# A fused linear-attention and FFN kernel: order of the opening's work, engine of the FFN weight's sums, and one bias addition a tile

## The reference, cut to what matters

```python
def _feature_map(x): return jax.nn.elu(x) + 1.0

# block 1: causal linear attention, 16 heads of 32, a running state kv and ksum per sequence
qkv = ln(x) @ W_attn + b_attn
q, k, v = split(qkv); q, k = _feature_map(q), _feature_map(k)
kv = kv + k[..., :, None] * v[..., None, :];  ksum = ksum + k     # token by token
y = (q . kv) / (q . ksum + 1e-6)
x = x + y @ W_proj + b_proj
# block 2: one linear layer on values rounded to fp8 e4m3
x = x + float16(fp8(ln(x))) @ float16(fp8(weight)).T + bias
```

## Time and profile before

| | |
|---|---|
| median of 3 runs | 955.94 us (952.33 to 960.21) |
| the profiled execution | 953.16 us |
| its span in the trace | 951.4 us |
| TensorE busy | 922.6 us (97%) |
| VectorE, ScalarE, GpSimd busy | 731.3, 747.3, 639.3 us |
| granted TensorE clock, mean | 0.998 |

### The profile page before, as it was taken

One profiled execution on the slowest core, in us unless ns is written; L12 is line 12 of the kernel. 1 busy time (PEld: TensorE's weight loads), 2 busy tenths in 40 slices (PEclk: granted clock), 3 DMA queues, 4 the chain that ended last, 5 costly groups with the idle time before them and its releaser, 6 DMA issues.

```text
span 951.4 us, 44839 instructions
## 1 busy us (share of the span) xinstructions
PE 922.6 (97%) x19533; PEld 491.2 (52%) x19533; DVE 731.3 (77%) x1405; ACT 747.3 (79%) x1362; POOL 639.3 (67%) x711
## 2 busy tenths in 40 slices
PE   7898999999999999999999999999999999999985
PEld 4354455555555555555555555555555555555553
DVE  7898778787786877778687687777778687676785
ACT  6787687887869688787877868788787868878864
POOL 5559777866767767776766777677676676654533
PEclk9999999999999999999999999999999999999999
DMA  8826554565464655564456555556566446553421
GB/s 270 139 44 116 96 119 94 101 119 93 100 125 93 100 119 96 98 119 98 99 116 106 93 113 109 100 104 113 90 109 115 95 103 120 90 93 70 69 71 51
DMA packets 252420, 99.12 MB, mean 104 GB/s; under 512 B 232384, under 2 KB 233408, under 8 KB 252224
## 3 DMA queue, kind: packets, MB, share of 16 engines
q1 hardware_dynamic: 252224, 96.25, 52.3%
HBM read 22.81 MB, written 16.78 MB: 42 GB/s over the span
## 4 chain that ended last, share of the span: by engine, by line
PE 87%; DVE 5%; POOL 2%; issue 2%; ACT 2%; SPq 1%; DMA 1%; POOLq 0%; DVEq 0%; ACTq 0%
PE R L245 74%; PE S L245 13%; DVE st L665 1%; DVE raw L704 1%; POOL st L944 1%; SPq L1168 1%; DVE qk L681 1%; POOL xn L946 1%; DMA yt<-yhl 0%; POOL xs L991 0%; DVE v L693 0%; POOL raw L977 0%; PE R L249 0%; DMA x2t<-x2b 0%; DVE wl L807 0%
## 5 line engine op out<-in xcount | busy, mean ns | idle before, releaser
L245 PE MATMUL R<-xt,wh 128*128 128x512 f16 x1024 | 304.6, 379 | 3.6 <-ACT rel L469 2.7
L681 DVE SCALAR_TENSOR_TENSOR qk<-qk,rel 128x512 f32<-128x512 f32 x128 | 112.9, 884 | 121.1 <-ACT rel L469 121.1
L457 ACT ACTIVATE raw<-qk 64x512 f32<-64x512 f32 x256 | 160.8, 628 | 49.2 <-PE S L245 46.0
L245 PE MATMUL R<-xt,wl 128*128 128x512 f16 x512 | 193.6, 379 | 0.0
L998 POOL TENSOR_TENSOR yhl<-y,yhl 128x512 f16<-128x512 f32 x60 | 70.1, 1168 | 146.4 <-ACT yhl L457 146.3
L245 PE MATMUL R<-wh,xt 128*128 128x512 f16 x512 | 158.0, 379 | 0.7 <-issue 0.7
L944 POOL TENSOR_TENSOR st<-st,half 128x1 f32<-128x1 f32 x128 | 94.1, 735 | 96.0 <-DVE st L670 95.4
L704 DVE TENSOR_TENSOR raw<-S,causal 64x1024 f32<-64x1024 f32 x128 | 155.8, 1217 | 2.0 <-PE S L245 1.1
L245 PEld LDWEIGHTS R<-xt,wh 128*128 128x128 f16 x1024 | 96.2, 98 | 116.7 <-ACT rel L469 3.4
L245 PE MATMUL R<-wph,yt 128*128 128x512 f16 x512 | 132.0, 380 | 5.1 <-ACT yt L457 3.2
L466 ACT ACTIVATE qk<-R,bqk,wm 128x512 f32<-128x512 f32 x128 | 98.8, 772 | 32.5 <-PE R L245 32.0
(11 more groups left out here) (95 smaller groups left out, 1410.3 us busy)
## 6 DMA issues: line engine op xcount, KB each, us to landing
xs<-in_L_attn_x SPq DMA_DIRECT2D x64, 256.0 KB, 3.3
out<-xs SPq DMA_DIRECT2D x64, 256.0 KB, 2.4
raw<-in_L_attn_W_attn SPq DMA_DIRECT2D x2, 1024.0 KB, 9.5
raw<-in_L_attn_W_attn SPq DMA_DIRECT2D x2, 512.0 KB, 5.7
xs<-in_L_attn_W_proj SPq DMA_DIRECT2D x4, 256.0 KB
raw<-in_L_ffn_weight SPq DMA_DIRECT2D x1, 1024.0 KB, 17.3
raw<-raw SPq DMA_TRANSPOSE x63, 3.7
x2t<-x2b SPq DMA_TRANSPOSE x62, 2.5
```

The lines of the kernel that those rows point to most:

```text
L245: return e.matmul(out, a, b, start=start, stop=stop, skip_group_check=True)
L457: return e.activation(out, in_, ACT.Copy, **more)
L681: e.scalar_tensor_tensor(qk[j % 2][:, i, :], qk[j % 2][:, i, :], 1.0, rel[:, (u - 1) % 2, :], ALU.min, ALU.add).then_inc(s_phi, 1)
```

## The change

It has five parts; no value that is computed changes.

1. VectorE's `ln1(5)` and then `ln1(6)` stand one step earlier (`ln1(5)` ahead of `v_peak`), and GpSimd's `ln1(5)` ahead of its `ln1_parts(4)`.
2. VectorE's `v_scale()` stands behind phi(0, 5) to phi(0, 7) instead of ahead of them.
3. `most(4)` on TensorE, `proj_scale()` on VectorE and `proj_weight()` on ScalarE move from ahead of tile 0's first two chunks to behind them, VectorE's `proj_weight()` behind values(0), and `ffn_round()` from tile 0 to tile 1.
4. The FFN weight's four sums move from VectorE to GpSimd in tile 1, with a semaphore of their own (`s_wfs`); SP issues the first two `wft` transposes ahead of `yt` of tile 1 and the other two behind it.
5. `add_bp`: before, GpSimd did tiles n + 8 and n in each of tiles 0 to 7, and n + 8 alone from then on; now tile n in every tile n.

```diff
-XB_ORDER = (*(m for n in range(8) for m in (n + 8, n)), *range(16, NT))
...
     @block.tensor
...
             for i in range(12):
                 proj_qkv(0, i)
-                if i in (1, 4, 11):
-                    most((1, 4, 11).index(i) + 2)
+                if i in (1, 4):
+                    most((1, 4).index(i) + 2)
...
                     ahead(chunks(n)[0])
+                    if n == 0:
+                        most(4)
...
     @block.scalar
...
                     if n == 0:
                         spread(n)
-                        proj_weight()
                     if n >= 2 and not tail(n):
                         t2(n - 2)
                     ahead(chunks(n)[0])
+                    if n == 0:
+                        proj_weight()
...
     @block.vector
...
-                dve.wait_ge(s_xb, xb_count(n))
+                dve.wait_ge(s_xb, n + 1)
...
             ln1(4)
             attn_weight(4)
+            ln1(5)
             phi(0, 1)
             v_peak()
             attn_weight(5)
             phi(0, 2)
-            ln1(5)
             scale(3)
             phi(0, 3)
+            ln1(6)
             attn_weight(6)
-            ln1(6)
             phi(0, 4)
             attn_weight(7)
             ln1(7)
-            v_scale()
             phi(0, 5)
             phi(0, 6)
             phi(0, 7)
+            v_scale()
             v_out(0, 0)
...
             update(0)
-            proj_scale()
             for n in range(NT + 2):
...
                     if n + 8 < NT:
                         ln1(n + 8)
+                    if n == 1:
+                        ffn_round()
+                    ahead(chunks(n)[0])
                     if n == 0:
-                        proj_weight()
-                    if n == 1:
-                        ffn_sum(0, 2)
-                    ahead(chunks(n)[0])
+                        proj_scale()
...
                     values(n)
                     if n == 0:
+                        proj_weight()
                         ffn_high()
-                        ffn_round()
                         ahead(chunks(n)[1])
...
-                if n == 1:
-                    ffn_sum(2, 4)
...
     @block.gpsimd
...
+            def ffn_sum(f):
+                pool.wait_ge(s_wfd, 3)
+                e.tensor_tensor(w_b[:, f, :], w_hi[:, f, :], w_lo[:, f, :], ALU.add).then_inc(s_wfs, 1)
...
             ln1(4)
+            ln1(5)
             ln1_parts(4)
-            ln1(5)
             ln1_parts(5)
...
                     if n == 0:
                         values(n)
-                    elif n + 8 < NT:
-                        add_bp(n + 8)
+                    else:
+                        add_bp(n)
...
+                    if n == 1:
+                        ffn_sum(0)
+                        ffn_sum(1)
                     if n:
                         values(n)
-                    if 1 <= n < 8:
-                        add_bp(n)
+                    if n == 1:
+                        ffn_sum(2)
+                        ffn_sum(3)
...
                 if n == 0:
-                    add_bp(n + 8)
                     add_bp(n)
...
     @block.sync
...
+            def t_wf(f):
+                sp.wait_ge(s_wfs, f + 1)
+                e.dma_start(wft[:, :, f * P:(f + 1) * P], w_b[:, f, :], transpose=True).then_inc(s_wft, 16)
...
                 if n == 1:
+                    t_wf(0)
+                    t_wf(1)
                     t_y(n)
-                    for f in range(4):
-                        sp.wait_ge(s_wfd, 4 + f)
-                        e.dma_start(wft[:, :, f * P:(f + 1) * P], w_b[:, f, :], transpose=True).then_inc(s_wft, 16)
+                    t_wf(2)
+                    t_wf(3)
```

More of the change, by code:

```diff
@@ L193, in build @@
         s_rs1, s_xn, s_rs2, s_x2, s_xb, s_x1b = sem("rs1"), sem("xn"), sem("rs2"), sem("x2"), sem("xb"), sem("x1b")
-        s_yl, s_blank, s_one, s_khl, s_near = sem("yl"), sem("blank"), sem("one"), sem("khl"), sem("near")
+        s_wfs, s_yl, s_blank, s_one, s_khl, s_near = sem("wfs"), sem("yl"), sem("blank"), sem("one"), sem("khl"), sem("near")
         bank = {}
@@ L851, in ffn_round @@
                                 saturate=False).then_inc(s_wfd, 1)
-            def ffn_sum(first, end):
-                dve.wait_ge(s_wfd, 3)
-                for f in range(first, end):
-                    e.tensor_tensor(w_b[:, f, :], w_hi[:, f, :], w_lo[:, f, :], ALU.add).then_inc(s_wfd, 1)
             e.memset(pair[:, :], 0.0).then_inc(s_pair, 1)
```

2 lines of the change are left out of this document (removed).

## The result

| | before | after |
|---|---|---|
| median of 20 runs each | 955.45 us | 959.3 us |
| ratio of the runs | | 1.0037, 95% interval 1.0025 to 1.0049 |
| profiled execution, span | 953.16, 951.4 us | 954.91, 953.2 us |
| granted TensorE clock, mean of the profiled execution | 0.998 | 0.993 |
| values(0), (1), (2), (3) start | 57.37, 71.98, 85.41, 103.55 | 55.68, 75.67, 89.01, 103.58 |

A forecast was written before the change was run, and what follows sets the result against it. TensorE's own work was taken to bound the middle, leaving only its opening idle time to win. Removed 7.29 us less 3.8 left or new gave 3.5 us gain, so a median of 952.4 us; range 948.5 to 957.5.

The forecast's parts named there:

- 7.29 us of waits: TensorE's three idle times in the opening, at 31.71, 44.60 and 92.33 us; taken as the ceiling of the gain.
- 3.8 us left or new: Waits expected in the opening: 0.5 for first v_out, 2.2 for k_tokens(1), 1.1 from x2(0) and y.
- all 2.41 us go: Opening, 31.71 us: with x5's statistics earlier, TensorE's whole 2.41 us wait for a Relu disappears.
- the last join ends near 39 … the 2.23 us go: Opening, 44.60 us: with v_scale behind the joins, TensorE's 2.23 us wait for VectorE's last join disappears.
- new wait that I put at 0.5: Twelfth chunk: v_out, started near 41.7, ends at 43.2, but its bank is wanted at 42.7; 0.5 us wait.
- TensorE waits 2.2 us in update(1): Tile 1: ScalarE's W_proj split ahead of k_tokens(1) makes TensorE wait 2.2 us, leaving a lead of some 2 us.
- 4.3 us … (2.41 + 2.23 - 0.5, rounded): values(0): TensorE reaches it near 53.1 instead of 57.37, 4.3 us ahead.
- 1.16 … I take that: Tile 1: each FFN weight sum on GpSimd takes 1.16 us, the time of GpSimd's subtraction of two 128x512 inputs.
- x2(0) ends at 82.9: Tile 1, GpSimd: x2 of tile 0 is normed by 82.9, 0.5 us before the earlier 83.44.
- scores(3) starts at 90.4: Tile 3: scores(3) starts at 90.4 instead of 93.97, with y ready then; 3.5 us gained.
- In tiles 56 to 63 GpSimd has one addition of bp more …, but it waits there anyway …: nothing.: Tail: an extra bp addition a tile (1.3 us each) falls into GpSimd's waiting time, so costs nothing.
- The slower rival: Tile 1: GpSimd becomes the bound if sums take 2.0 us or more; scores(3) 2.2 us later, 958.1 us; chance 0.14.

The follow-up runs named there:

- f2_bias_alone: Kernel before with only the new order of the bp additions (tile n in every tile n); 957.62 us, ratio 1.0031.
- h2_scale_behind: Kernel before with only v_scale moved behind the last three joins; 957.36 us, ratio 1.0010.
- g4_split_alone: Kernel before with only W_proj's maximum, scale and split moved as in the change, ffn_round not moved; 957.88 us, ratio 1.0037.
- e2_split_back: Changed kernel with W_proj's maximum, scale and split back ahead of tile 0, ffn_round left in tile 1; 955.81 us, ratio 1.0001.
- e1_bias_back: Changed kernel with the old order of the bp additions (tiles n + 8 and n in tiles 0 to 7); 958.28 us, ratio 1.0024 to the kernel before.
- h1_bias_moved: Changed kernel with the bp additions of tiles 57 to 63 moved on GpSimd ahead of x2's norm; 960.76 us, ratio 1.0051 to the kernel before.
- e4_fill: Changed kernel with 11 identity transposes on TensorE ahead of update(1)'s wait, filling half of it; 961.73 us, ratio 1.0065 to the kernel before.

## Why the prediction was wrong

By the profiled executions my sum comes out like this. Of the 7.29 us of waits 6.29 went (1.81, 1.83 and 2.65). Where I had 3.8 us left or new, there were 0.93 for v, 2.45 for ktok and 2.8 behind that wait, 6.2 together; that leaves 0.1 for the opening, where I had 3.5. And where I had nothing for the tail, it lost 1.6. The term that decides is part 3's: undoing it alone takes the ratio from 1.0037 to 1.0001.

*Part 1, "all 2.41 us go".* 1.81 did; right in place, and 1.1 us in time when run alone, with an interval that reaches zero.

*Part 2, "the last join ends near 39 … the 2.23 us go", v_out at 41.7.* This step failed. I moved v_scale past three joins and counted their VectorE time, but not that the last join waits for a Relu: VectorE idled 2.71 us with v_scale behind it, and v_out came at 44.25. The Relu in turn stood on ScalarE behind the high part of x7, whose norm on GpSimd ended at 38.75. Alone the part brings nothing (1.0010). The new wait that I put at 0.5 was 0.93.

*Part 3, "TensorE waits 2.2 us in update(1)".* This step failed too, and it weighs most. 2.45: the size of the wait was right. What I set against it was wrong. I took the 2.2 as half of a lead given back, after which the chain goes on as it was. It is a part with no gain of its own and a cost of 0.37% alone, at a clock of 1.00 in the opening. And in the changed kernel there came behind the wait what the prediction did not have at all, a granted clock of 0.50 and a longer issue gap, 2.8 us together in the profiled execution. (The lead of "4.3 us … (2.41 + 2.23 - 0.5, rounded)" is 4.1 by its own terms; it was 1.7.)

*Parts 4 and 5, the sums: "1.16 … I take that".* 1.08; right. "x2(0) ends at 82.9" was wrong, it was 85.7: my values(0) was at 53.1, where it was 55.68, so the split of W_proj began at 58.86 and not 56.0, and everything on GpSimd in tile 1 hangs on that. (0.55 of the 2.6 us are the trace's late start.) ffn_round took 1.22 us and not 2.06, which gave 0.8 back. So "scores(3) starts at 90.4" came at 94.59. I had also credited the part with the earlier x2t. Alone it costs 0.19%, through the row of v behind x2(0)'s norm, which my count did not have among the waiters.

*"In tiles 56 to 63 GpSimd has one addition of bp more …, but it waits there anyway …: nothing."* Wrong, and the plainest error. I looked at when GpSimd is idle and not at what it stops when it is not. The addition costs 1.24 us of VectorE's residual addition in each of two tiles and 0.31% alone. The Trainium skill, "SBUF — State Buffer", section "SBUF: two separate sides", which I cited for tile 1, has the shared port locked for a whole instruction and the other engine waiting. The rows agree with waiting, on either engine (GpSimd's norm at 875.71 waits as well), and at 899.99 they go beyond one instruction, to bf, bp and COPY on end. I had weighed it where VectorE's operations read PSUM, and not for the residual addition with its two SBUF operands.

*The slower rival.* It named the sign and GpSimd, and its place was tile 1 with sums of 2.0 us and more. The sums were 1.08. It came out slower by another mechanism in another place; that its sign was right is luck.

Single parts give +0.37, +0.31 and +0.19% for parts 3, 5 and 4, -0.11 for part 1 and +0.10 (open) for part 2. Their sum is 0.86%, the whole change 0.37. Each is known to some 0.15 only, so the sum to 0.35 or so; that the parts share waits, and so don't add, fits this but is not shown by it. What stays open is why the medians differ by some 2 us more than the two profiled executions, of which after's was its fastest. The mean granted clock over the runs is 0.9956 before (in the runs beside the experiments) and 0.9926 after. Among the runs of one kernel 0.001 less of it goes loosely with 0.26 us (before) to 0.49 us (after), so the clock would account for 0.8 to 1.5 us. Where it falls in the unprofiled runs no trace shows.

## What to carry to other kernels

When an instruction is moved behind others, ask of each of these what it waits for: an engine's idle time ahead of a waiting instruction is the place for work, and behind it the work comes that much later. Idle time of GpSimd says nothing of what its work costs when it does run: look for VectorE operations with two SBUF operands beside it, and read in the trace which of GpSimd's rows they wait out. That a pause between GpSimd's instructions would free them wasn't tried. A lead in the opening is kept only if each chain that ends in the next stage moves with it (here x2 of tile 0, the v row behind it, and SP's queue), so take the last of them first.

## What the hardware showed that I had not expected

- A VectorE addition of two SBUF operands, 0.68 us at its shortest, took 1.98, 3.23 and 4.73 us beside three, four and five instructions that GpSimd ran without a pause (a COPY row is two), and ended 0.54 to 0.55 us behind the last each time. Beside another unbroken row (887.30 in after) it was let in behind the first instruction.
- Behind a wait of TensorE the granted clock fell to 0.50 in some cases (2.45 us, after at 62.29; 2.37 us, f2_bias_alone at 915.92; 1.46 us, h2_scale_behind at 52.36) and not in others (2.62 us, g4_split_alone at 64.42; 2.36 us, after itself at 916.37; 1.46 us, e2_split_back at 50.95). All three kernels with both the lead and the wait of 2.45 to 2.62 us in update(1) have the fall there (after, e1_bias_back, h1_bias_moved). What decides it these runs don't show.
- Issue gaps of TensorE come and go: before has 0.90 us at 63.73, and f2_bias_alone, whose instructions on TensorE are the same in the same order, has none there. e4_fill has two in the middle, 1.77 us together, where the other fifteen traces have none (100 to 860 us, gaps over 0.15 us).
